# Cross attention on one core: probabilities times values for two groups of heads in a row, with a buffer of turned probabilities for every head

## The reference

```python
Q = split_heads(Query @ W_q.T)
K = split_heads(Key @ W_k.T)
V = split_heads(Value @ W_v.T)
scores = jnp.einsum('bhqd,bhkd->bhqk', Q, K) / jnp.sqrt(jnp.asarray(D_K, dtype=Q.dtype))
attn = jax.nn.softmax(scores, axis=-1)
X = jnp.einsum('bhqk,bhkd->bhqd', attn, V)
...
x = _layernorm(x + _L0_xattn_ref(x, ctx_1024, ctx_1024, mask_1x1xSxS2_if1, ...), axis=-1)
```

## Time and profile before

| | us |
|---|---|
| median of three runs | 2441.42 |
| profiled execution, its own time | 2437.63 |
| its span, first to last instruction | 2435.9 |
| PE busy in the whole span | 2197.9 (90%) |
| DVE, ACT busy | 1724.2 (71%), 1319.0 (54%) |

### The profile page before, as it was taken

One profiled execution on the slowest core, in us unless ns is written; L12 is line 12 of the kernel. 1 busy time (PEld: TensorE's weight loads), 2 busy tenths in 40 slices (PEclk: granted clock), 3 DMA queues, 4 the chain that ended last, 5 costly groups with the idle time before them and its releaser, 6 DMA issues. The chain is left out here.

```text
span 2435.9 us, 48613 instructions
## 1 busy us (share of the span) xinstructions
PE 2197.9 (90%) x15771; PEld 1853.4 (76%) x15771; DVE 1724.2 (71%) x4286; ACT 1319.0 (54%) x3188; POOL 513.9 (21%) x421
## 2 busy tenths in 40 slices
PE   8789999859999976898799999799999999999995
PEld 5578777747999965565678777678888888888884
DVE  2567777755888854777477778687776777768564
ACT  3257777744666634656477777444444444444441
POOL 3200000010111052322100000023333333333333
PEclk9889999979999997999799999899999999999997
DMA  4067666322766621000456666122322323222222
GB/s 116 3 147 137 130 126 128 80 75 90 230 200 210 186 67 37 1 0 0 118 129 139 130 129 138 56 80 84 106 93 95 106 77 113 88 97 93 70 76 68
DMA packets 201755, 246.50 MB, mean 101 GB/s; under 512 B 58481, under 2 KB 176706, under 8 KB 201602
## 3 DMA queue, kind: packets, MB, share of 16 engines
q1 hardware_dynamic: 198050, 235.37, 36.8%
q0 software_dynamic: 3552, 9.18, 1.3%
HBM read 202.95 MB, written 41.55 MB: 100 GB/s over the span
## 5 line engine op out<-in xcount | busy, mean ns | idle before, releaser
L843 ACT ACTIVATE cross_pr<-cross_sc,cross_mn 112x375 f32<-112x375 f32 x512 | 311.6, 609 | 188.9 <-DVE cross_mn L939 180.7
L2389 POOL TENSOR_TENSOR switch_gl<-switch_gb,switch_gh 128x896 fp32r<-128x896 f32 x128 | 270.9, 2117 | 572.9 <-ACT switch_gh L2570 572.9
L939 DVE CUSTOM_DVE_ANT_0 cross_sc<-cross_ps,cross_masked 112x375 f32<-112x375 f32 x512 | 272.9, 544 | 86.8 <-PE cross_ps L728 74.9
L736 PE MATMUL cross_ps<-all_ident,cross_pr 112*125 112x112 f32 x1536 | 255.7, 275 | 30.0 <-DVE cross_pt L946 28.7
L2626 DVE SCALAR_TENSOR_TENSOR switch_vt<-switch_ps,switch_chosen,switch_vt 112x128 f32<-112x128 f32 x512 | 144.1, 344 | 189.4 <-PE switch_ps L106 184.7
L736 PEld LDWEIGHTS cross_ps<-all_ident,cross_pr 112*125 112x125 f32 x1536 | 232.4, 189 | 51.1 <-DVE cross_pt L946 32.3
L728 PE MATMUL cross_ps<-cross_k,cross_q 96*112 96x376 f32 x512 | 214.7, 420 | 15.4 <-DMA cross_k<-cross_k_dram 11.7
L104 PE MATMUL switch_ps<-switch_vw,switchgates_xh 128*112 128x512 f32 x512 | 209.3, 409 | 4.9 <-ACT switch_vt L2549 4.9
L104 PE MATMUL switch_ps<-switch_gh,switch_ow 128*128 128x448 f32 x512 | 192.5, 376 | 18.0 <-POOL switch_gl L2389 16.7
L106 PE MATMUL switch_ps<-switch_vw,switchgates_xl 128*112 128x512 f32 x512 | 202.5, 395 | 0.0
L105 PE MATMUL switch_ps<-switch_vw,switchgates_xh 128*112 128x512 f32 x512 | 202.0, 395 | 0.0
(11 more groups left out here) (397 smaller groups left out, 5734.7 us busy)
## 6 DMA issues: line engine op xcount, KB each, us to landing
switch_gb<-switch_gt_rows SPq DMA_DIRECT2D x128, 448.0 KB, 3.6
experts_w_raw<-in_L_ffn_w_dram SPq DMA_DIRECT2D x42, 1024.0 KB, 5.6
cross_k<-cross_k_dram SPq DMA_DIRECT2D x96, 375.0 KB, 7.8
cross_k_dram<-cross_ks SPq DMA_DIRECT2D x32, 750.0 KB, 4.7
all_place<-in_ctx_dram SPq DMA_DIRECT2D x32, 375.0 KB
cross_q<-cross_q_dram SPq DMA_DIRECT2D x192, 56.0 KB, 4.4
all_place<-in_L_ffn_v_w_dram SPq DMA_DIRECT2D x16, 512.0 KB, 6.2
all_place<-in_L_ffn_o_w_dram SPq DMA_DIRECT2D x8, 1024.0 KB, 7.2
```

The lines of the kernel that those rows point to most:

```text
L736: last = nc.tensor.transpose(ps[0:KP, TURNED + h % 2, t * T:(t + 1) * T], pr[:, h % NB, t * KP:(t + 1) * KP], ident[0:T, 0:T])
L843: nc.scalar.activation(pr[:, h % NB, :], sc[:, h % NB, :], ACT.Exp, bias=mn[parity][:, h:h + 1], scale=-1.0, accum_out=rs[parity][:, h:h + ...
L939: nc.vector.tensor_tensor_reduce(out=sc[:, h % NB, :], in0=ps[0:T, SCORES + h % 2, 0:S2], in1=mask_of[:], scale=-0.25, scalar=3e38, op0=AL ...
L2389: pool.tensor_tensor(gl[u % 2][:], gb[u % RING][:], gh[u % 2][:].bitcast(F32), ALU.subtract)\
```

## The change

`pt` gets one buffer for each of the 16 heads. The groups 0 and 1 are both multiplied at step 12, one right behind the other, and the groups 2 and 3 both at step 4 of the next batch; nothing is multiplied at steps 8 and 0 any more. A copy into `pt` now waits for the group of the same heads one batch before.

```diff
-        pt = s.sb("pt", [KP, NB, KT * T])
+        pt = s.sb("pt", [KP, H, KT * T])
...
-        VALUES_AT, VALUES_OF_LAST = {8: 0, 12: 1}, {0: 2, 4: 3}
+        VALUES_AT, VALUES_OF_LAST = {12: (0, 1)}, {4: (2, 3)}
...
-                                                pt[:, h % NB, t * T:(t + 1) * T], start=t == 0, stop=t == KT - 1)
+                                                pt[:, h, t * T:(t + 1) * T], start=t == 0, stop=t == KT - 1)
...
                     if i in VALUES_AT:
-                        values(b, parity, VALUES_AT[i])
+                        for g in VALUES_AT[i]:
+                            values(b, parity, g)
                     elif i in VALUES_OF_LAST and not first:
-                        values(b - 1, 1 - parity, VALUES_OF_LAST[i])
+                        for g in VALUES_OF_LAST[i]:
+                            values(b - 1, 1 - parity, g)
...
-            for g in VALUES_OF_LAST.values():
+            for g in VALUES_OF_LAST[4]:
                 values(B - 1, 1, g)
...
-                wait(act, pv_done, b * QUADS + (h - NB) // QUAD + 1)
-                nc.scalar.copy(pt[:, h % NB, :], ps[0:KP, TURNED + h % 2, 0:KT * T]).then_inc(pt_act, 1)
+                wait(act, pv_done, (b - 1) * QUADS + h // QUAD + 1)
+                nc.scalar.copy(pt[:, h, :], ps[0:KP, TURNED + h % 2, 0:KT * T]).then_inc(pt_act, 1)
```

More of the change, by code:

```diff
@@ L944, in evacuate @@
                 dve.wait_ge(t_done, b * H + h + 1)
-                wait(dve, pv_done, b * QUADS + (h - NB) // QUAD + 1)
-                nc.vector.tensor_copy(pt[:, h % NB, :], ps[0:KP, TURNED + h % 2, 0:KT * T]).then_inc(pt_dve, 1)
+                wait(dve, pv_done, (b - 1) * QUADS + h // QUAD + 1)
+                nc.vector.tensor_copy(pt[:, h, :], ps[0:KP, TURNED + h % 2, 0:KT * T]).then_inc(pt_dve, 1)
             def tail(b, parity, part, ch):
```

## The result

The changed kernel took 2480.36 us, the median of four runs (2477.59 to 2482.9), against 2440.77 before: a ratio of 1.0162 with a 95% interval of 1.0145 to 1.018. It is slower by some 40 us, where I had forecast 4.4 and a range that ended at 2452.

A forecast was written before the change was run, and what follows sets the result against it. The bound was taken to be a ring in which PE and DVE wait for each other in turn. 0.66 - 0.49 = +0.17 us a batch, times 26 = +4.4, edges 0, on 2441.42 gave 2446 us, range 2437 to 2452.

The forecast's parts named there:

- The ring: In a cross attention batch PE and DVE wait for each other in turn; the change adds 0.17 us a batch.
- What one more group costs behind another: PE time of a second group right behind a first: 0.66 us, ends 0.52 and 0.88.
- Step 0, gain 0: Group 2 gone: PE reaches the turn of head 14 up to 0.88 us earlier but waits for DVE; gain 0.
- Step 4, +0.66: Groups 2 and 3 together end later, and DVE's `V0` with them: +0.66 us a batch.
- Step 8, 0.49 given back: Group 0 gone: scores of head 9 are ready for DVE, whose idle time falls away; 0.49 us given back.
- Step 12, cost 0: Groups 0 and 1 together fit into PE's wait for DVE; cost 0, at most 0.2 us.
- Buffers and waits, cost 0: The copies into `pt` wait for a group that ended a batch ago; cost 0.
- Rival A: PE is the bound and each of some 58 joins saves 0.22 us: -12.8, so 2429 us; chance 0.12.
- Rivals B and C: Nothing given back at step 8 (2459, chance 0.05); second group as dear as one alone (2450 to 2452, chance 0.13).
- rival D: PE's clock falls as its idle time at step 1 grows to over 1 us; several us if so, chance 0.02.

The follow-up runs named there:

- late pair: Changed kernel with groups 0 and 1 back at steps 8 and 12, groups 2 and 3 still both at step 4; 2489.69 us, ratio 1.0209.
- early pair: Changed kernel with groups 2 and 3 back at steps 0 and 4, groups 0 and 1 still both at step 12; 2427.13 us, ratio 0.9948.
- group 2 left out: Changed kernel with the groups back at their old steps and group 2 (heads 8 to 11) never multiplied; 2481.42 us, ratio 1.0168.
- group 2 twice: Changed kernel with group 2 multiplied once more at step 0, its result written over at step 4; 2442.87 us, ratio 1.0012.
- `V0` moved: Changed kernel with PE's part of `V0` at step 0 instead of step 2; 2442.65 us, ratio 1.001.

## Why the prediction was wrong

**The ring was right.** The forecast was +0.17 us a batch from the waits. The changed kernel with its clock held up measures +0.10 to +0.16, batch 1 of the changed kernel +0.16. By its places:

- *What one more group costs behind another:* 0.66 was taken, 0.58 measured. The pair at the stage's end, from which it was read, had been kept apart by ACT's last copy by more than the 0.03 that I took off.
- *Step 0, gain 0:* right as to the ring. The late pair alone pays for step 4 and gets nothing for step 0 (+0.56 to +0.62 in its batches at clock 1.00).
- *Step 4, +0.66:* the same +0.56 to +0.62.
- *Step 8, 0.49 given back:* the early pair alone gives 0.48.
- *Step 12, cost 0:* right, the early pair shows it.
- *Buffers and waits, cost 0:* 1.0008, right.
- *Rival A, the joins pay:* a join does make PE's work shorter, by 0.88 less 0.58. The Trainium skill's rule in "TensorEngine Tiling (Array Packing)", section "Key Properties", that a change of mode drains the engine, agrees with these rows in direction; they do not show the drain itself. But PE's saving did not set the end: the late pair has its join and got slower, and the early pair gained what DVE's wait at step 8 had held, 0.48.

- *Rivals B and C:* out. The give-back at step 8 is there, and the pair costs less than I took, in the loop too.

**The step that failed is rival D, the clock.** I gave it 0.02 and excused it with the stage's end, where PE is busy 11.87 of 15 us at clock 1.00. That row is a mean over 15 us, and so says little of the one place at which idle time piles up. The right question was put in the prediction itself: "PE's wait grows by what was removed. Gain: 0." I took idle time that nothing waits for as free. The row to compare was PE's busy time in the last steps before the turn of head 14: 1.96 of 2.4 us before. Taking a group of 0.88 out leaves 1.1, and that is what the run shows (1.12). The term that failed is thus the cost of PE's idle time at step 0 and 1, put at nothing; it cost about 1.4 us a batch (36 us over 26 batches). What follows at half clock is no slack either: steps 2 to 4 are the part of the ring that PE leads, so the loss goes straight into `V0` of DVE and into the batch.

The size follows from the rows: a stretch of 3.4 us at half clock does the work of 1.7, so it costs 1.7 us where PE leads. 25 stretches make 42 us. The measured excess of the changed kernel over the one with the filled step 0 is 37.5 us, or 36 if each is taken against its own kernel before. That the rest fell on moments at which PE would have waited anyway is likely, and not shown.

That a fall needs this idle time, and not the pair, is shown by six kernels: it comes with step 0 empty (changed kernel, late pair, group 2 left out) and goes with it filled (early pair, group 2 twice, `V0` moved). The idle time alone is not enough, though: in the changed kernel PE is busy only 1.03 to 1.33 of the 2.4 us ahead of the turn of head 14 in all 28 batches 1 to 14, and 3 of these kept their clock. The Trainium skill, "TensorE: Matmul & The Clock Gate", section "Part 1: The HAM clock gate (the "warmup" mystery)", describes TensorE's clock as passed at half or full rate by how busy the engine has been of late. The trace agrees with both levels, 0.50 and 1.00. I had weighed the Trainium skill's rule on tiling, which speaks for the change, and not this one, which speaks against it.

What stays open: why some batches with the same idle time keep their clock (3 of 28 in the changed kernel, 6 of 28 with group 2 left out), and how much of step 0 has to be filled; only a group of 0.88 and a `V0` of some 0.7 us were tried.

## What to carry to other kernels

On TensorE, work that stands in a wait can be dear to take away: before removing or moving it, look at PE's busy time in the few us that end at that wait, and at how dense PE's work is behind it. Where a change leaves a hole there, move other work of PE into it, and read the granted clock of that stretch, not of the stage. And a change with two halves should be costed, and run, as two: here one half was worth 12 us and the other cost 50.

## What the hardware showed that I had not expected

- The clock fell at a place where PE's matmuls had stood idle for 0.86 us in one piece and its weight loads for 1.11, in the batch shown, in a stage where PE is busy 92% of the time (43.91 of 47.63 us). It fell to 0.50 and came back after 3.4 us, in 25 of 28 batches. Over these 28 the idle piece of the matmuls was between 0.68 and 1.36 us, and batches with 1.13 and 1.31 kept the clock.
- A kernel got slower by 1.7% from leaving out 12 matmuls a batch, and the changed kernel got faster by 1.5% (2480.36 to 2442.87) from computing 12 of them twice.
- Two groups of column-tiled matmuls in a row, with two semaphore waits between, run without a break: 24 records more take 0.58 us (1.36 less 0.78), while one among other work costs 0.88.
